# Folding four states at a time, in a selective-scan kernel of 16 layers

## The chip, the cores and the metric

The kernel runs on one core of a Trainium2 chip. The metric is the device time of one execution in microseconds (us); it is 16410.44 us as the median of three runs (16390.57 to 16411.66).

## The reference

Images are embedded as patches (16 x 16 pixels with four shifted copies), joined with text tokens to 16 sequences of 324 tokens with 192 features, and normed. Then come 16 Mamba layers, a shared expert, and a mixture of 16 experts. The change touches only the layers. One layer, cut to what is computed:

```
h = rmsnorm(x) * w;  u, z = split(in_w @ h)               # 384 channels each
u = silu(causal_conv(u) + b)                               # 4 taps, per channel
dt_r, Bm, Cm = split(x_proj @ u)                           # 48, 16, 16
dt = softplus(dt_proj @ dt_r + dt_b);  A = -exp(A_log)     # A: 384 channels x 16 states
for t: h = exp(dt_t * A) * h + dt_t * u_t * B_t            # 16 states per channel
       y_t = sum over n of h[:, n] * C_t[n]  + u_t * D
x = x + out_w @ (y * silu(z))
```

## The kernel before

A **unit** is one sequence in one layer; there are 16 x 16 = 256, and `UNITS` of them run in a loop, two a turn. The recurrence is laid out with 128 partitions = 32 channels x 4 states and 972 elements = 3 x 324 tokens (`IT` x `L`). So a unit is 16 **steps** n = 0 to 15. I call the tile of step s "state s", as the code does; it holds 128 (channel, state) pairs, and four consecutive steps s use the strips r = s mod 4 of the output partitions.

Each step has this chain, one engine after the other:

- ScalarE, **decay** (`se_decay`, line 596): three exponentials from `dt_rep` into a bank pair of PSUM; two such buffers, so decay s waits for scan s - 2.
- GpSimd, **dbu** (`ge_dbu`, 814): `dtu_rep` times `b_rep`; four buffers, so dbu s waits for scan s - 4.
- VectorE, **scan** (`ve_scan`, 764): the recurrence along the tokens into one of eight tiles `h`.
- **product** with C: on VectorE with C from PSUM (`ve_product`, 773) one step later, or for the states in `ON_POOL` on GpSimd with C from SBUF (`ge_product`, 821), issued after dbu s + 4.
- PE, **sum** (`te_sum`, 449): a matmul with the 128 x 32 matrix `fold` adds 128 rows to 32 output partitions of `y_ps`. One call takes two states, so two of the four strips.

Beside it, every engine carries the projections of later units, which a planner of fixed places puts into the steps: for unit u the z projection of u + 1 (`te_z`, 478), the u projection (`te_u`, 513), convolution (`te_conv`, 527), x projection (`te_xp`, 547) and dt projection (`te_dt`, 556) of u + 2, and the squares for the norm of u + 3 (`te_ss`, 539). They share one PSUM bank `pj`, so each waits until ScalarE has evicted the one before: z (line 620), u (632), convolution (639), x (683), dt (691, 692). `te_skip` (465) adds u * D into `y_ps`; `te_bcast` (435) writes the C rows of four states over all partitions for the products. `ve_gate` (781) multiplies `y_ps` with silu(z) when all sums of a unit are in; `te_out` (493, 495) is the output projection, evicted at 626. `ve_log_error` (788) and three GpSimd operations (834 to 842) finish softplus.

Every engine runs its queue in the order in which `tensor_step`, `scalar_step`, `vector_step`, `gpsimd_step` and `sync_step` write it, by step n; waits are semaphores. ScalarE at n = 12 loads an activation table, does the SiLU of u and z, and loads the first table back (647, 653, 655); at n = 1 it loads another for two logarithms and returns (725, 729). In `tensor_step` the eight sums of a unit stand at the places `SUM_AT`: the pairs (0,1), (2,3), ... (12,13) at n = 3, 6, 7, 10, 11, 14, 15, and (14,15) at n = 1 of the next unit. The two halves of the skip stand at n = 7 and 10, the output projection at 3 and 4, the u projection at 5 and 6.

Of the kernel before, what the change touches and what calls it, by code (L numbers as in the profile page):

```python
# [35 lines left out]
DRING = 4  # L36
ON_POOL = (3, 7, 11)
EPS = 1e-5
# [263 lines left out]
LOG_SET = "natural_log"  # L302
FREED = 2 + RING + 1 + 1 + 2 + 1


def run_layers(nc, cst, x_T, params, weights, b_rows, dt_rows, dtu_rows):

    ident, ones96, sel_c, fold = cst["ident"], cst["ones96"], cst["sel_c"], cst["fold"]
    with ExitStack() as ctx:
# [112 lines left out]
        def by_vector(u, s):  # L422

            return (N - len(ON_POOL)) * u + sum(i not in ON_POOL for i in range(s + 1)) + 1

        def by_pool(u, s):

            return len(ON_POOL) * u + sum(i in ON_POOL for i in range(s + 1))

# [6 lines left out]

        def te_sum(pe, u, m):

            if m >= -1:
                reached(pe, s_prod, by_vector(u, 2 * m + 1))  # L440
            if 2 * m + 1 in ON_POOL:
                reached(pe, s_pprod, by_pool(u, 2 * m + 1))
            if m == 0:
                reached(pe, s_gate, u + 1)
            for half in range(2):
                for s in (2 * m, 2 * m + 1):
                    r = s % NR
                    src = h[s % RING][:, :, :].rearrange("p i t -> p (i t)")
                    mm = pe.matmul(y_ps[32 * r:32 * r + 32, half, :], fold[:, :], src[:, half * YW:(half + 1) * YW],  # L449
                                   start=(m in (0, 1)), stop=(m % 8 in (6, 7)))  # L450
            mm.then_inc(s_sum, 1)
# [29 lines left out]

        def te_out(pe, u, half, lone=False):

            if half == 0:
                reached(pe, s_gate, u + 1)
                wait(pe, s_wo, 16 * ((u + B - 1) // B + 1))
                if lone:
                    reached(pe, s_dtev, 2 * u + 4)
                else:
                    reached(pe, s_zev, 2 * u + 4)  # L490
            else:
                reached(pe, s_oev, 2 * u + 1)
# [6 lines left out]
        def te_u(pe, k, par, half, scan, b1):  # L499
            if half == 0:  # L500
                reached(pe, s_xn, k + 1)
                wait(pe, s_wu, 16 * (layer(k) + 1))
                if scan:
                    reached(pe, s_oev, 2 * k - 2)
                elif b1:
                    reached(pe, s_zev, 2 * k)
                else:
                    reached(pe, s_lnss, k + 2)
            else:
                reached(pe, s_ur, 2 * k + 1)  # L510
            for it, lo, hi, t in pieces(half):
                for c in range(2):
                    mm = pe.matmul(pj[:, lo:hi], w_u[:, c, it * 128:it * 128 + 128], x_norm[par][:, c, t:t + hi - lo],  # L513
                                   start=(c == 0), stop=(c == 1))
            mm.then_inc(s_u, 1)

        def te_conv(pe, k, half):

            if half == 0:
                wait(pe, s_wc, 16 * (layer(k) + 1))  # L520
                reached(pe, s_ur, 2 * k + 2)
            else:
                reached(pe, s_cvev, 2 * k + 1)
# [36 lines left out]

        SUM_AT = (3, 6, 7, 10, 11, 14, 15, 1)

        def tensor_step(pe, u, par, scan=True, a1=True, b1=True):

            p, k, j = u + 1, u + 2, u + 3
            for n in range(N):
                if scan and n % 4 == 1:
                    te_bcast(pe, u, par, n // 4)
                if n == 0:
                    te_ss(pe, j, b1)  # L570
                if n in (1, 2) and b1:
                    te_z(pe, p, 1 - par, n - 1)
                if n in (3, 4) and scan:
                    te_out(pe, u, n - 3)
                if n in (5, 6) and a1:
                    te_u(pe, k, par, n - 5, scan, b1)
                if n in (8, 9) and a1:
                    te_conv(pe, k, n - 8)
                if n == 12 and a1:
                    te_xp(pe, k, par)  # L580
                if n in (13, 14) and a1:
                    te_dt(pe, k, n - 13)
                for m in (i for i, at in enumerate(SUM_AT) if scan and at == n):
                    te_sum(pe, u, m if n != 1 else -1)
                if n in (7, 10) and scan:
                    te_skip(pe, u, par, (n - 7) // 3)

# [125 lines left out]
        def scalar_step(act, u, par, scan=True, a1=True, b1=True):  # L713
# [5 lines left out]
            for n in range(N):  # L719
# [15 lines left out]
                if n == 2 and b1:  # L735
                    se_softplus(act, p, 2)
                if n in (4, 5) and scan:
                    se_out(act, u, n - 4)
                if n == 4 and b1:
                    se_c_rows(act, p, other)  # L740
                if n == 5 and a1:
                    se_copy_cb(act, k)
                if n in (6, 7) and a1:
                    se_ur(act, k, n - 6)
                if n == 6:
# [30 lines left out]
        def ve_gate(dve, u, par):  # L776

            reached(dve, s_sum, 8 * u + 2)
            reached(dve, s_za, u)
# [11 lines left out]
        def vector_step(dve, u, par, scan=True, a1=True, b1=True):  # L791
            p = u + 1
            other = 1 - par
            for n in range(N):
                if scan:
                    ve_scan(dve, u, n)
                if n == 2 and scan:
                    ve_gate(dve, u, other)
                if scan:
                    if n - 1 not in ON_POOL:  # L800
                        ve_product(dve, u, n - 1)
                if n == 3 and b1:
                    ve_log_error(dve, p)
# [13 lines left out]
        def ge_product(pool, u, s):  # L817

            wait(pool, s_cr[s // NR], 16 * (u + 1))
            reached(pool, s_scan, 16 * u + s + 1)  # L820
            pool.tensor_tensor(h[s % RING][:, :, :], h[s % RING][:, :, :],  # L821
                               c_rep[:, s // NR, :].unsqueeze(1).broadcast_to([128, IT, L]), ALU.mult).then_inc(s_pprod, 1)

# [36 lines left out]
        def sp_store_b(sp, k, par):  # L860
            reached(sp, s_xpev, k + 1)
            for s in s_bq + s_cr:
                wait(sp, s, 16 * (k - 1))
            sp.dma_start(b_rows[par], xp_rows[96:128, :]).then_inc(s_bst, 16)

# [6 lines left out]

        def sp_load_c(sp, u, par, q):
            reached(sp, s_pprod, len(ON_POOL) * u + q + 1)
            sp.sem_inc(s_go, 1)
            wait(sp, s_bst, 16 * (u + 2))
            sp.dma_start(c_rep[:, q, :], b_rows[1 - par, N + 4 * q:N + 4 * q + 4, :].unsqueeze(0).broadcast_to([32, 4, L])
                         ).then_inc(s_cr[q], 16)

# [87 lines left out]
        with nc.Block() as block:  # L967
            @block.sync
            def _(sp):
# [52 lines left out]
                sp.wait_ge(s_bst, 16 * (UNITS + 2))  # L1022
                for s in s_bq + s_cr + s_dtr + s_dur + s_dst:
                    sp.wait_ge(s, 16 * (UNITS + 1))
                sp.wait_ge(s_wu, 16 * (NL + 1))
                sp.wait_ge(s_wc, 16 * (NL + 1))
# [44 lines left out]
            def _(pool):  # L1071
                raise_counts(pool, s_dbu, s_dt, s_xn, s_pprod)
# [780 lines left out]
```

## Time and profile before

| | |
|---|---|
| median of the runs | 16410.44 us |
| the profiled execution's own time | 16389.14 us |
| its span | 16387.3 us |
| PE matmul busy | 13833.0 us, 84% |
| VectorE (DVE) busy | 13770.8 us, 84% |
| GpSimd (POOL) busy | 13369.5 us, 82% |
| ScalarE (ACT) busy | 11352.2 us, 69% |
| mean granted TensorE clock | 0.889 of full |

Times of rows are microseconds from the start of the span. A row of a timeline is a group of like instructions that follow each other: start, duration, engine, source line, operation, output <- inputs, shapes, count; in brackets stands how long the engine had been idle before it and what released it. A float32 matmul call shows as two matmul instructions. Instructions of one engine overlap by about 0.08 us, so starts are the better measure than durations. Matmul ends are modelled.

### The profile page before, as it was taken

How to read it: one execution, taken by the hardware profiler on the slowest of the kernel's cores; microseconds unless marked ns; L12 is line 12 of the kernel's file. 1: busy time of each engine (PE TensorE's matmuls, PEld its weight loads, DVE VectorE, ACT ScalarE, POOL GpSimd, SP SyncE). 2: the span in 40 equal slices, each digit the busy share in tenths (PEclk: the TensorE clock that was granted, in tenths of full speed). 3: DMA queues.
4: the chain of work that ended last, by engine and by line, in shares of the span. 5: the costliest groups of instructions: out<-in, count | busy, mean ns of one | idle time of the engine just before them, and what ended most of it. 6: DMA issues, size and time to landing. Idle time of an engine off the chain costs nothing. (4 is left out here: it accounts for less than half of the span.)

```text
span 16387.3 us, 204104 instructions
## 1 busy us (share of the span) xinstructions
PE 13833.0 (84%) x52202; PEld 6844.4 (42%) x52202; DVE 13770.8 (84%) x9806; ACT 11352.2 (69%) x21632; POOL 13369.5 (82%) x6093
## 2 busy tenths in 40 slices
PE   6888888888888888888888888888888888887689
PEld 4344444444443444444444444443443444444367
DVE  2899899989998998999899899989998998994643
ACT  3777777777777777777777777777777777774111
POOL 1999999999999999999999999999999999990023
PEclk7888888988999998888888988989998888887799
DMA  2333333333333333333333333333333333331022
GB/s 71 117 110 110 110 118 106 114 114 115 107 114 116 110 109 113 116 106 114 115 113 108 113 116 110 109 113 115 106 114 116 112 108 114 115 110 40 11 51 58
DMA packets 714623, 1703.38 MB, mean 104 GB/s; under 512 B 89050, under 2 KB 369607, under 8 KB 714307
## 3 DMA queue, kind: packets, MB, share of 16 engines
q1 hardware_dynamic: 693810, 1685.70, 30.8%
q0 software_dynamic: 19968, 15.98, 0.6%
q14 instruction: 109, 0.89, 0.0%
q10 hardware_dynamic: 720, 0.55, 0.0%
q8 instruction: 16, 0.26, 0.0%
HBM read 1415.12 MB, written 286.74 MB: 104 GB/s over the span
## 5 line engine op out<-in xcount | busy, mean ns | idle before, releaser
L814 POOL TENSOR_TENSOR dbu<-dtu_rep,b_rep 128x972 f32<-128x972 f32 x4096 | 9140.3, 2250 | 1307.6 <-DVE h L764 1282.5
L764 DVE TENSOR_TENSOR_SCAN h<-ps,dbu 128x972 f32<-128x972 f32 x4096 | 8851.4, 2171 | 1073.8 <-ACT ps L596 1072.5
L596 ACT ACTIVATE ps<-dt_rep,A_cur 128x323 f32<-128x323 f32 x12288 | 5882.9, 521 | 1015.7 <-DVE h L764 752.5
L449 PE MATMUL ps<-h,fold 128*32 128x486 f32 x16400 | 4221.9, 696 | 97.9 <-DVE h L773 53.0
L773 DVE TENSOR_TENSOR h<-h,ps 128x972 f32<-128x972 f32 x3329 | 3797.1, 1141 | 1.2 <-PE ps L435 1.2
L449 PEld LDWEIGHTS ps<-h,fold 128*32 128x32 f32 x16400 | 881.1, 125 | 2694.5 <-issue 2173.1
L821 POOL TENSOR_TENSOR h<-h,c_rep 128x972 f32<-128x972 f32 x768 | 1961.8, 2554 | 0.0
L527 PE MATMUL ps<-u_raw,w_cv 128*128 128x162 f32 (+7 forms) x8256 | 1802.5, 372 | 96.2 <-ACT u_pre L639 94.7
L527 PEld LDWEIGHTS ps<-u_raw,w_cv 128*128 128x128 f32 x8256 | 1348.0, 190 | 525.9 <-ACT u_pre L639 227.1
L556 PE MATMUL ps<-xp_rows,w_dt 49*128 49x162 f32 (+1 forms) x2064 | 808.3, 529 | 660.2 <-ACT dt L692 334.2
L478 PE MATMUL ps<-x_norm,w_z 96*128 96x324 f32 (+1 forms) x4112 | 1320.9, 481 | 1.4 <-ACT rstd L665 0.7
L435 PE MATMUL ps<-c_rows,sel_c 16*128 16x324 f32 x2048 | 835.7, 488 | 524.8 <-DVE h L773 523.7
L1611 POOL DMA_INDIRECT e_rows<-n_rows,e_ix x96 | 96.9, 1010 | 1301.4 <-issue 1205.7
L513 PE MATMUL ps<-x_norm,w_u 96*128 96x324 f32 (+1 forms) x4128 | 989.2, 383 | 193.2 <-ACT u_raw L632 187.4
L478 PEld LDWEIGHTS ps<-x_norm,w_z 96*128 96x128 f32 x4112 | 869.7, 244 | 631.3 <-issue 557.7
L495 PE MATMUL ps<-y_gated,w_o 128*96 128x324 f32 x3084 | 925.8, 436 | 0.0
L513 PEld LDWEIGHTS ps<-x_norm,w_u 96*128 96x128 f32 x4128 | 666.3, 191 | 508.3 <-ACT u_raw L632 251.0
L556 PEld LDWEIGHTS ps<-xp_rows,w_dt 49*128 49x128 f32 x2064 | 425.1, 242 | 941.9 <-ACT xp_rows L683 459.5
L626 ACT COPY x_T<-ps 96x324 f32 (+1 forms) x514 | 218.2, 424 | 835.1 <-PE ps L495 835.1
L547 PE MATMUL ps<-u_act,w_x 128*128 128x324 f32 x1548 | 491.4, 454 | 359.9 <-ACT u_act L647 352.9
L435 PEld LDWEIGHTS ps<-c_rows,sel_c 16*128 16x128 f32 x2048 | 300.3, 183 | 941.7 <-DVE h L773 663.9
L639 ACT COPY u_pre<-ps 128x486 f32<-128x486 f32 x516 | 288.2, 559 | 545.7 <-PE ps L527 545.7
(170 smaller groups left out, 14767.0 us busy)
## 6 DMA issues: line engine op xcount, KB each, us to landing
dtu_rep<-dtu_rows SPq DMA_DIRECT2D x1028, 486.0 KB, 3.9
dt_rep<-dt_rows SPq DMA_DIRECT2D x1028, 486.0 KB, 6.5
b_rep<-b_rows SPq DMA_DIRECT2D x1028, 162.0 KB, 2.6
dt_rows<-dt SPq DMA_DIRECT2D x257, 486.0 KB, 2.7
dtu_rows<-dtu SPq DMA_DIRECT2D x257, 486.0 KB, 2.7
c_rep<-b_rows SPq DMA_DIRECT2D x771, 162.0 KB, 5.6
w_cv<-in_w_cv SPq DMA_DIRECT2D x17, 768.0 KB, 7.6
b_rows<-xp_rows SPq DMA_DIRECT2D x258, 40.5 KB, 6.4
```

Of the source, the lines that this page charges most:

```text
L435: pe.matmul(c_ps, sel_c[64:80, q, :], c_rows[par][64:80, :], start=True, stop=True).then_inc(s_cbc, 1)
L449: mm = pe.matmul(y_ps[32 * r:32 * r + 32, half, :], fold[:, :], src[:, half * YW:(half + 1) * YW], start=(m in (0, 1)), stop=(m % 8 in (6, ...
L478: mm = pe.matmul(pj[:, lo:hi], w_z[:, c, it * 128:it * 128 + 128], x_norm[par][:, c, t:t + hi - lo], start=(c == 0), stop=(c == 1))
L495: mm = pe.matmul(pj[0:HC, 0:L], w_o[:, it, half * HC:(half + 1) * HC], y_gated[:, it, :], start=False, stop=(it == IT - 1))
L513: mm = pe.matmul(pj[:, lo:hi], w_u[:, c, it * 128:it * 128 + 128], x_norm[par][:, c, t:t + hi - lo], start=(c == 0), stop=(c == 1))
L527: mm = pe.matmul(pj[:, lo + skip:hi], w_cv[:, it * KC + KC - 1 - back, :], u_raw[:, it * L + t + skip - back:it * L + t + hi - lo - back], ...
L556: mm = pe.matmul(pj[:, lo:hi], w_dt[:, it * 128:it * 128 + 128], xp_rows[0:RB, t:t + hi - lo], start=True, stop=True)
L596: ins = act.activation(decay[s % 2][:, it * L + 1:(it + 1) * L], dt_rep[:, s % NR, it, 1:L], ACT.Exp, scale=A_cur[:, it * N + s:it * N + s ...
L764: dve.tensor_tensor_scan(h[s % RING][:, :, :].rearrange("p i t -> p (i t)"), decay[s % 2], dbu[s % DRING][:, :, :].rearrange("p i t -> p ( ...
L773: dve.tensor_tensor(h[s % RING][:, :, :], h[s % RING][:, :, :], c_ps.unsqueeze(1).broadcast_to([128, IT, L]), ALU.mult).then_inc(s_prod, 1)
L814: pool.tensor_tensor(dbu[s % DRING][:, :, :], dtu_rep[:, r, :, :], b_rep[:, q, :].unsqueeze(1).broadcast_to([128, IT, L]), ALU.mult).then_ ...
L821: pool.tensor_tensor(h[s % RING][:, :, :], h[s % RING][:, :, :], c_rep[:, s // NR, :].unsqueeze(1).broadcast_to([128, IT, L]), ALU.mult).t ...
```

## The change

One sum now takes four states, all four strips, at n = 6, 10, 13 and at n = 2 of the next unit, so four calls with eight matmuls instead of eight with four. GpSimd makes the products of states 1, 5 and 13 instead of 3, 7 and 11; the last is made in the next unit. The u projection (n = 3, 4) goes ahead of the output projection (n = 5, 6); both halves of the skip run at n = 7. The gate stands after scan 3 instead of scan 2, the log error after product 3. ScalarE's evictions and the loads of C move along.

```diff
-ON_POOL = (3, 7, 11)
+ON_POOL = (1, 5, 13)
...
-        def te_sum(pe, u, m):
-
-            if m >= -1:
-                reached(pe, s_prod, by_vector(u, 2 * m + 1))
-            if 2 * m + 1 in ON_POOL:
-                reached(pe, s_pprod, by_pool(u, 2 * m + 1))
-            if m == 0:
+        def te_sum(pe, u, q):
+
+            reached(pe, s_prod, by_vector(u, 4 * q + 3))
+            if (4 * q + 1) % N in ON_POOL:
+                reached(pe, s_pprod, by_pool(u, 4 * q + 1))
+            if q == 0:
                 reached(pe, s_gate, u + 1)
             for half in range(2):
-                for s in (2 * m, 2 * m + 1):
-                    r = s % NR
-                    src = h[s % RING][:, :, :].rearrange("p i t -> p (i t)")
+                for r in range(NR):
+                    src = h[(4 * q + r) % RING][:, :, :].rearrange("p i t -> p (i t)")
                     mm = pe.matmul(y_ps[32 * r:32 * r + 32, half, :], fold[:, :], src[:, half * YW:(half + 1) * YW],
-                                   start=(m in (0, 1)), stop=(m % 8 in (6, 7)))
+                                   start=(q == 0), stop=(q < 0))
...
-        def te_out(pe, u, half, lone=False):
+        def te_out(pe, u, half, a1=True, b1=True):
...
-                if lone:
+                if a1:
+                    reached(pe, s_ur, 2 * u + 6)
+                elif b1:
+                    reached(pe, s_zev, 2 * u + 4)
+                else:
                     reached(pe, s_dtev, 2 * u + 4)
-                else:
-                    reached(pe, s_zev, 2 * u + 4)
...
-                if scan:
-                    reached(pe, s_oev, 2 * k - 2)
-                elif b1:
+                if b1:
                     reached(pe, s_zev, 2 * k)
...
-        def te_conv(pe, k, half):
+        def te_conv(pe, k, half, scan):
 
             if half == 0:
+                if scan:
+                    reached(pe, s_oev, 2 * k - 2)
...
-        SUM_AT = (3, 6, 7, 10, 11, 14, 15, 1)
-
...
+                if n in (2, 6, 10, 13) and scan:
+                    te_sum(pe, u, (n - 6) // 4 if n < 13 else 2)
                 if n in (1, 2) and b1:
                     te_z(pe, p, 1 - par, n - 1)
-                if n in (3, 4) and scan:
-                    te_out(pe, u, n - 3)
-                if n in (5, 6) and a1:
-                    te_u(pe, k, par, n - 5, scan, b1)
+                if n in (3, 4) and a1:
+                    te_u(pe, k, par, n - 3, b1)
+                if n in (5, 6) and scan:
+                    te_out(pe, u, n - 5, a1, b1)
+                if n == 7 and scan:
+                    te_skip(pe, u, par, 0)
+                    te_skip(pe, u, par, 1)
...
-                for m in (i for i, at in enumerate(SUM_AT) if scan and at == n):
-                    te_sum(pe, u, m if n != 1 else -1)
-                if n in (7, 10) and scan:
-                    te_skip(pe, u, par, (n - 7) // 3)
...
-                if n in (4, 5) and scan:
-                    se_out(act, u, n - 4)
+                if n in (6, 7) and scan:
+                    se_out(act, u, n - 6)
...
-                if n in (6, 7) and a1:
-                    se_ur(act, k, n - 6)
+                if n in (4, 5) and a1:
+                    se_ur(act, k, n - 4)
...
-            if s % 2 == 0:
-                reached(dve, s_sum, 8 * u + s // 2 - 1)
+            if s % 4 == 0:
+                reached(dve, s_sum, 4 * u + s // 4)
...
-                if n == 2 and scan:
+                if n == 3 and scan:
                     ve_gate(dve, u, other)
...
-                if n == 3 and b1:
+                if n == 4 and b1:
                     ve_log_error(dve, p)
...
-                    if n - 4 in ON_POOL:
-                        ge_product(pool, u, n - 4)
+                    if (n - 4) % N in ON_POOL:
+                        ge_product(pool, u if n >= 4 else u - 1, (n - 4) % N)
...
-        def sp_load_c(sp, u, par, q):
-            reached(sp, s_pprod, len(ON_POOL) * u + q + 1)
+        def sp_load_c(sp, u, par, at):
+
+            s = ON_POOL[at]
+            reached(sp, s_pprod, by_pool(u - 1, s))
             sp.sem_inc(s_go, 1)
-            wait(sp, s_bst, 16 * (u + 2))
...
+            wait(sp, s_bst, 16 * (u + 1))
...
             p = u + 1
+            if scan:
+                sp_load_c(sp, u, par, len(ON_POOL) - 1)
             for q in range(NQ):
...
-                for q in range(len(ON_POOL)):
-                    sp_load_c(sp, u, par, q)
+                for at in range(len(ON_POOL) - 1):
+                    sp_load_c(sp, p, 1 - par, at)
...
+                pool.memset(c_rep[:, :, :], 0.0).then_inc(s_free, 1)
                 pool.wait_ge(s_free, FREED)
                 all_units(gpsimd_step, pool)
+                ge_product(pool, UNITS - 1, ON_POOL[-1])
```

## Rows read from the trace of the kernel before

**Rows 1.** The gate's line over the whole span: its instructions and their idle time.

```profile
L781 DVE TENSOR_TENSOR y_gated<-ps,z_act x257: 1169/1171/1172, 377.3 to 14785.9; 128x972 f32<-128x972 f32 x129
...
  PE ps L449: 358.4, 251
```

**Rows 2.** Timeline of VectorE, end of one unit and start of the next.

```profile
8001.78 1.14 DVE L773 TENSOR_TENSOR h<-h,ps 128x972 f32<-128x972 f32 x1
8002.84 2.17 DVE L764 TENSOR_TENSOR_SCAN h<-ps,dbu 128x972 f32<-128x972 f32 x1
8004.93 1.14 DVE L773 TENSOR_TENSOR h<-h,ps 128x972 f32<-128x972 f32 x1
...
8014.93 2.18 DVE L764 TENSOR_TENSOR_SCAN h<-ps,dbu 128x972 f32<-128x972 f32 x1 [3.62 <-ACT ps L596]
...
8035.64 1.17 DVE L781 TENSOR_TENSOR y_gated<-ps,z_act 128x972 f32<-128x972 f32 x1 [2.65 <-PE ps L449]
...
8037.80 2.17 DVE L764 TENSOR_TENSOR_SCAN h<-ps,dbu 128x972 f32<-128x972 f32 x1
...
8040.95 2.39 DVE L788 SCALAR_TENSOR_TENSOR dtu<-u_pre,dtu 128x972 f32<-128x972 f32 x1
```

**Rows 3.** Timeline of ScalarE over the same stretch.

```profile
8005.85 1.44 ACT L596 ACTIVATE ps<-dt_rep,A_cur 128x323 f32<-128x323 f32 x3
8008.47 1.28 ACT L647 ACT_TABLE_LOAD   x1 [1.18 <-PE ps L465]
...
8016.68 0.58 ACT L691 ACTIVATE exp_x<-ps 128x486 f32<-128x486 f32 x1
...
8019.43 0.57 ACT L691 ACTIVATE exp_x<-ps 128x486 f32<-128x486 f32 x1 [0.38 <-PE ps L556]
...
8021.40 1.44 ACT L596 ACTIVATE ps<-dt_rep,A_cur 128x323 f32<-128x323 f32 x3 [0.80 <-DMA dt_rep<-dt_rows]
...
8029.25 1.44 ACT L596 ACTIVATE ps<-dt_rep,A_cur 128x323 f32<-128x323 f32 x3
8032.05 0.56 ACT L620 COPY z_pre<-ps 128x486 f32<-128x486 f32 x1 [1.37 <-PE ps L478]
...
8033.98 1.43 ACT L596 ACTIVATE ps<-dt_rep,A_cur 128x323 f32<-128x323 f32 x3
```

**Rows 4.** Timeline of PE matmuls, the same unit and the next.

```profile
8013.31 0.81 PE L435 MATMUL ps<-c_rows,sel_c 16*128 16x324 f32 x2
8015.40 1.08 PE L556 MATMUL ps<-xp_rows,w_dt 49*128 49x324 f32 x4 [1.28 <-ACT xp_rows L683]
...
8028.41 3.61 PE L478 MATMUL ps<-x_norm,w_z 96*128 96x324 f32 x8
8031.95 3.45 PE L449 MATMUL ps<-h,fold 128*32 128x486 f32 x8
...
8038.03 0.78 PE L493 MATMUL ps<-x_T,ident 96*96 x2 [0.79 <-ACT z_pre L620]
...
8040.38 1.83 PE L449 MATMUL ps<-h,fold 128*32 128x486 f32 x8
...
8072.58 1.79 PE L556 MATMUL ps<-xp_rows,w_dt 49*128 49x324 f32 x4 [1.23 <-ACT xp_rows L683]
...
8077.59 4.42 PE L449 MATMUL ps<-h,fold 128*32 128x486 f32 x16
```

**Rows 5.** Windows: length, busy us of PE, PEld, DVE, ACT, POOL; granted clock; DMA.

```profile
8011.50:8018.10 6.60, 4.03 (x14) 2.32 (x15) 3.17 (x3) 6.56 (x13) 6.60 (x4) 1.00 0.78 245
8018.30:8021.50 3.20, 3.20 (x11) 0.84 (x13) 3.20 (x3) 2.02 (x6) 3.20 (x3) 0.50 0.92 333
...
8025.00:8028.40 3.40, 0.73 (x2) 0.29 (x2) 3.40 (x3) 3.35 (x5) 2.50 (x2) 1.00 0.23 71
8028.50:8035.20 6.70, 6.70 (x16) 2.85 (x16) 4.45 (x3) 5.32 (x11) 6.70 (x4) 0.50 0.00 0
```

**Rows 6.** Timeline of GpSimd, its longest wait of the unit.

```profile
8040.05 2.26 POOL L814 TENSOR_TENSOR dbu<-dtu_rep,b_rep 128x972 f32<-128x972 f32 x1 [4.57 <-DVE h L764]
```

More of the change, by code:

```diff
@@ L302 @@
 LOG_SET = "natural_log"
-FREED = 2 + RING + 1 + 1 + 2 + 1
+FREED = 2 + RING + 1 + 1 + 2 + 1 + 1
 def run_layers(nc, cst, x_T, params, weights, b_rows, dt_rows, dtu_rows):
@@ L422, in by_vector @@
         def by_vector(u, s):
+            if s < 0:
+                return by_vector(u - 1, s + N)
             return (N - len(ON_POOL)) * u + sum(i not in ON_POOL for i in range(s + 1)) + 1
         def by_pool(u, s):
-            return len(ON_POOL) * u + sum(i in ON_POOL for i in range(s + 1))
+            if s < 0:
+                return by_pool(u - 1, s + N)
+            return len(ON_POOL) * u + sum(i in ON_POOL for i in range(s + 1)) + 1
         def te_bcast(pe, u, par, q):
@@ L497, in te_out, with te_u @@
             mm.then_inc(s_out, 1)
-        def te_u(pe, k, par, half, scan, b1):
+        def te_u(pe, k, par, half, b1):
             if half == 0:
@@ L570, in tensor_step @@
                     te_ss(pe, j, b1)
+                if n in (2, 6, 10, 13) and scan:
+                    te_sum(pe, u, (n - 6) // 4 if n < 13 else 2)
                 if n in (1, 2) and b1:
                     te_z(pe, p, 1 - par, n - 1)
-                if n in (3, 4) and scan:
-                    te_out(pe, u, n - 3)
-                if n in (5, 6) and a1:
-                    te_u(pe, k, par, n - 5, scan, b1)
+                if n in (3, 4) and a1:
[5 more added lines that the diff above has]
+                    te_skip(pe, u, par, 1)
                 if n in (8, 9) and a1:
-                    te_conv(pe, k, n - 8)
+                    te_conv(pe, k, n - 8, scan)
                 if n == 12 and a1:
@@ L776, in ve_gate @@
         def ve_gate(dve, u, par):
-            reached(dve, s_sum, 8 * u + 2)
+            reached(dve, s_sum, 4 * u + 1)
             reached(dve, s_za, u)
@@ L817, in ge_product @@
         def ge_product(pool, u, s):
-            wait(pool, s_cr[s // NR], 16 * (u + 1))
+            at = ON_POOL.index(s)
+            reached(pool, s_cr[at], 16 * (u + 1))
             reached(pool, s_scan, 16 * u + s + 1)
             pool.tensor_tensor(h[s % RING][:, :, :], h[s % RING][:, :, :],
-                               c_rep[:, s // NR, :].unsqueeze(1).broadcast_to([128, IT, L]), ALU.mult).then_inc(s_pprod, 1)
+                               c_rep[:, at, :].unsqueeze(1).broadcast_to([128, IT, L]), ALU.mult).then_inc(s_pprod, 1)
         def ge_x_norm(pool, j, par):
@@ L861, in sp_store_b @@
             reached(sp, s_xpev, k + 1)
-            for s in s_bq + s_cr:
+            for s in s_bq:
                 wait(sp, s, 16 * (k - 1))
+            for s in s_cr:
+                sp.sem_inc(s_go, 1)
+                reached(sp, s, 16 * (k - 1))
+                sp.sem_inc(s_go, 1)
             sp.dma_start(b_rows[par], xp_rows[96:128, :]).then_inc(s_bst, 16)
@@ L871, in sp_load_b @@
                          ).then_inc(s_bq[q], 16)
-        def sp_load_c(sp, u, par, q):
-            reached(sp, s_pprod, len(ON_POOL) * u + q + 1)
+        def sp_load_c(sp, u, par, at):
+            s = ON_POOL[at]
+            reached(sp, s_pprod, by_pool(u - 1, s))
             sp.sem_inc(s_go, 1)
-            wait(sp, s_bst, 16 * (u + 2))
-            sp.dma_start(c_rep[:, q, :], b_rows[1 - par, N + 4 * q:N + 4 * q + 4, :].unsqueeze(0).broadcast_to([32, 4, L])
-                         ).then_inc(s_cr[q], 16)
+            wait(sp, s_bst, 16 * (u + 1))
+            n = N + s // NR * 4
+            sp.dma_start(c_rep[:, at, :], b_rows[par, n:n + 4, :].unsqueeze(0).broadcast_to([32, 4, L])
+                         ).then_inc(s_cr[at], 16)
         def sp_store_dt(sp, p, which):
@@ L1022, in _ @@
                 sp.wait_ge(s_bst, 16 * (UNITS + 2))
-                for s in s_bq + s_cr + s_dtr + s_dur + s_dst:
+                for s in s_bq + s_dtr + s_dur + s_dst:
                     sp.wait_ge(s, 16 * (UNITS + 1))
+                for s in s_cr[:-1]:
+                    reached(sp, s, 16 * (UNITS + 1))
+                reached(sp, s_cr[-1], 16 * UNITS)
                 sp.wait_ge(s_wu, 16 * (NL + 1))
@@ L1038, in _ @@
                               start=True, stop=False)
-                te_sum(pe, 0, -2)
                 all_units(tensor_step, pe)
                 te_sum(pe, UNITS, -1)
-                te_out(pe, UNITS, 0, lone=True)
-                te_out(pe, UNITS, 1, lone=True)
+                te_out(pe, UNITS, 0, a1=False, b1=False)
+                te_out(pe, UNITS, 1, a1=False, b1=False)
             @block.scalar
@@ L1071, in _ @@
             def _(pool):
-                raise_counts(pool, s_dbu, s_dt, s_xn, s_pprod)
+                raise_counts(pool, s_dbu, s_dt, s_xn, s_pprod, *s_cr)
                 for i in range(2):
```

## The prediction

> **What bounds the kernel now.** I read the page's engine shares first: PE, DVE and POOL are all busy for most of the span and none of them always, so the question is who waits for whom inside one unit (one sequence in one layer; there are 256). The gate product on line 781 runs once a unit, and its first and last start put the mean unit at (14785.9 - 377.3) / 256 = 56.28 us [rows 1]. All of the change lies in this stretch, 14409 us of the 16387 us span.
>
> Next the timeline of VectorE [rows 2]. A scan follows its predecessor's start by 2.09 us if nothing holds it (8002.84 to 8004.93), a product by 1.06 us (8001.78 to 8002.84), gate and one product take 2.16, the log error 2.32 (its 2.39 less the same overlap). Without a wait a unit is 16 x 2.09 + 13 x 1.06 + 1.08 + 2.32 = 50.6 us. The other 5.7 us are waits in two places: scan 13 waits 3.62 us for ScalarE's decay 13, and the gate waits for the fold sum, 2.65 us in this unit and 358.4 / 257 = 1.4 us on average [rows 1, 2].
>
> Then ScalarE's own queue between them [rows 3]: decay 12, table load, SiLUs, table load, decay 13, decays 14 and 15 with the dt evictions between, decay 0 of the next unit, softplus and logarithm, decay 2, the z eviction, decay 3. So I cut the unit at two marks: **E**, the end of scan 10 (8002.84 + 2.17 = 8005.01), and the start of the next unit's scan 3 (8037.80). From scan 3 to E VectorE has no wait: 8 x 2.09 + 5 x 1.06 + 2.32 = 24.3 us. From E to scan 3, which I call X, it took 32.8 us here, and 56.28 - 24.34 = 31.9 on average. In X ScalarE is the longer queue, so X is what the change must shorten.
>
> **The part from scan 3 to E, after.** The gate now follows scan 3 (+1.08), and of products 2 to 8 VectorE does six instead of five (+1.06), since 3 and 7 come back from GpSimd and 5 goes there: 26.5 us. This is 2.1 us more, and it comes off X, as the number of products a unit is still 13 and 3. The part stays without waits if ScalarE keeps up. The output projection now stands behind broadcast 1, which waits for product 3, and ScalarE holds decay 7 back until its first half is evicted. One output half takes PE 8040.38 - 8038.03 = 2.4 us [rows 4]. From scan 3: product 3 ends at 7.5, broadcast to 8.2, the output half to 10.7, its eviction and the weighted x to 12.2, decay 7 to 13.6. Scan 7 is due at 14.9, so 1.3 us are left. I cost it at nothing; at half clock the output half would take twice as long and cost about 1 us.
>
> **X, after, step by step, from E = 0.**
> 1. Decay 12 started 0.84 us after E, behind the second convolution eviction [rows 3]. Product 7 on VectorE gives the convolution 1.06 us more between scans 8 and 10, so this 0.84 goes.
> 2. The table load at 8008.47 waited 1.18 us for the skip matmuls of line 465 [rows 3]. Both halves of the skip now run at n = 7, directly behind the output projection and ahead of the convolution, and the convolution ends before E. The wait goes; it would be back only if the skip came later than the convolution does.
> 3. Decay 13 ended at 8014.91 (scan 13 starts at 8014.93). New: 14.91 - 5.01 - 0.84 - 1.18 = 7.9. VectorE is due at scan 13 after products 9, 10, 11 and scans 11, 12: 3 x 1.06 + 2 x 2.09 = 7.4. The stall falls from 3.6 to 0.5 us, and it is 11 returning to VectorE that fills a third of it.
> 4. What is late next is the dt projection. It is queued on PE behind broadcast 3 and the sum of states 8 to 11, both of which wait for product 11 on VectorE; before, product 11 was GpSimd's, the broadcast went at 8013.31 and the sum came later [rows 4]. Product 11 ends at 7.4, the broadcast takes it to 8.25 (0.81 less overlap), the sum to 10.0, dt half 0 (1.08) to 11.1. ScalarE is ready for it at 16.68 - 5.01 - 2.02 = 9.65. A new wait of 1.45 us on ScalarE; behind it stand decay 15, decay 0 and all that follows. Decay 15 ends at 13.5, scan 15 was due at 13.2.
> 5. Old waits that this swallows: 0.38 us for dt half 1 and 0.80 us for the dt_rep transfer [rows 3]; the transfer is still issued behind dbu 15, which was not moved, and decay 0 now comes at 14.5 instead of 16.4 less the 2.0 of steps 1 and 2, so it may keep a few tenths of its wait. From decay 0 to the end of decay 2: 29.25 + 1.44 - 21.40 = 9.3, so 23.8.
> 6. The z eviction: old wait 1.37 us, with z at half clock (3.61 us) [rows 3, 4]. Scan 0 starts at 16.65, product 15 ends at 19.9, broadcast to 20.7, z half 0 to 24.3: wait 0.5; with a broadcast at half clock 1.0; at full clock none (half of 3.61). From there to the end of decay 3: 33.98 + 1.43 - 32.05 = 3.4.
> 7. So decay 3 is ready at 27.2 at full clock, at 27.7 to 28.2 with z at half clock. The old gate wait is gone from X: the sum -1 is twice as many states, but has until scan 3 has ended; at half clock it ends near 27.8 against a gate at 30.
>
> X + 26.5 is the unit: **53.7 us** at full clock throughout, **54.5 us** with z at half clock, against 56.28.
>
> **The sum of four strips** has no row of its own. The nearest: a sum of two states, eight instructions, takes 1.83 us at full clock and 3.45 at half [rows 4]. If strips overlap only in pairs, sixteen take twice that; if all four do, once. The row at 8077.59 holds two sums on different pairs of strips, sixteen instructions in 4.42 us at half clock, the second begun about a microsecond late: four strips did run together. I take 1.83 and 3.45, and keep 3.66 and 6.9 for the range. PE so loses 4 x 1.83 = 7.3 us of work a unit, which by itself buys nothing, as PE was not last in X.
>
> **The clock.** Granted clock is 0.50, 1.2 GHz, in 8018.3 to 8021.5 and in 8028.5 to 8035.2. Before the first, PE was busy 4.03 of 6.60 us, before the second 0.73 of 3.40 [rows 5]. After the change PE does nothing from the sum of states 4 to 7 (ends near E + 1) to the x projection (E + 4.5), and only one group before E + 7.4; then it idles again from about 14 to 20, as the sums of states 10 to 13 no longer stand there. So z should be at half clock in nearly each unit, and the dt stretch in some. Now dt half 0 is seen at 1.08 us in one unit and at 1.79 in the next [rows 4]; there it cost nothing. If all of step 4 is at half clock: broadcast 1.2, sum 3.45, dt 1.8, so 13.9 instead of 11.1, product 15 and z go along, X = 31.0 and the unit 57.5. If the clock comes back within the sum, about 56.3. I take 56.8 as the mean of such units, and one unit in three: (2 x 54.5 + 56.8) / 3 = 55.3.
> The Trainium skill (TensorE: Matmul & The Clock Gate, Why this matters for your kernels) says that pauses between bursts of matmuls bring the engine back to half rate, and asks to keep it occupied. It speaks against taking work off PE ahead of the dt projection; the trace agrees as far as rows 5 go. By that rule taken strictly all units would be the 57.5 of the third rival below.
> The same page (Part 3, What overlaps and what doesn't) has matmuls start and end in program order. If PE could pull dt half 0 ahead of the sum instead, step 4 would have no wait and the unit would be nearer 53. In every row here PE keeps its order, so the sum goes by order.
>
> **The rest.** SP's load of C for state 13 now heads its step and waits for GpSimd's product 13 of the unit before; behind it stands the load of B's first rows, which waits for dbu 3, made later on GpSimd anyway: nothing. Three C loads a unit, as before. GpSimd makes 16 + 3 + 3 operations of 2.2 us and one of 1.6 either way, 50 us, and idled 4.57 us before the dbu at 8040.05 [rows 6]: with a unit of 55 us it still has 4 to 5. The log error still starts 1 us behind the dbu that overlaps it, so I leave it at 2.39; without GpSimd beside it it could be 1.2 us shorter, and behind a late dbu 1 us longer. The extra memset and the last product are some 5 us once.
>
> **Sum.** (55.27 - 56.28) x 256 = -259 us, +5: 16389 - 254 = 16135 us against the profiled execution, which lies 21 us under the median of the runs shown. **Predicted 16140 us.**
>
> **Rivals.**
> - **Clock stays up** (or z is never late): 53.7 a unit, -660 us, 15730. For it: the four-strip sum is dense work. Against: the two pauses.
> - **Strips overlap in pairs only**: step 4 becomes 1.8 us longer, the unit 56.3 to 56.6, 16390 to 16480: no change. Against it stands 8077.59.
> - **Slower: dt behind the sum at half clock in most units.** The wait of ScalarE between decays 14 and 15 grows from 1.45 to 4.3 us; it decides once that wait and the z wait together pass about 4.1 us (X = 29.8), which is when more than two units in three have it. 57 to 57.6 a unit: 16570 to 16730.
> - **GpSimd or the output projection becomes last** from scan 3 to E: up to 1.5 us a unit on top, 16140 to 16520.
>
> **Chances.** Forecast (15900 to 16330) 0.43, clock up 0.14, pairs 0.09, slower by dt 0.26, GpSimd or output 0.08. Faster by over 0.2% (33 us, about what a measurement tells from none): 0.39 + 0.14 + 0.02 + 0.05 = 0.60. Slower: 0.02 + 0.04 + 0.25 + 0.02 = 0.33. Within: 0.07. Range for 8 in 10: from just inside the full-clock case, 15790, to half-way into the slow rival, 16640; the forecast's own range is 15900 to 16330.
>
> **What would show it.** Idle before scan 13 about 0.5 us; no wait of the table load of line 647 on line 465; a new wait of ScalarE's line 691 on line 556, 1.4 us or up to 4; no wait before the gate; scans 2 and 3 waiting for line 596 instead; sixteen instructions of line 449 in about 1.9 us; mean granted clock of the layers below 0.89. The prediction is wrong if line 691's wait is near 4 us throughout, or if the gate or scan 4 still waits for PE, or if products 1, 5 and 13 hold a sum up.

## The result, and the profile after

The change made the kernel slower: 16629.99 us as the median of four runs (16615.15 to 16633.19), against 16407.94 us before (four runs, 16390.57 to 16411.66). The ratio is 1.0136, with a 95% interval of 1.0118 to 1.0153. The prediction was 16140 us with a range to 16640; it had faster at 0.60 and slower at 0.33. The time lies inside the range, 10 us from its upper end, and on the wrong side.

The gate's line, as in [rows 1], gives the mean unit: (15010.2 - 383.1) / 256 = 57.14 us against 56.28. That is +0.86 x 256 = 220 us, nearly all of 16631.4 - 16387.3 = 244.

```profile
L784 DVE TENSOR_TENSOR y_gated<-ps,z_act x257: 1142/1144/1170, 383.1 to 15010.2; 128x972 f32<-128x972 f32 x129
...
  PE ps L451: 3.6, 1
```

The gate wait is gone (358.4 us before, 3.6 now). The page's group of the scans (busy, mean ns, idle before them and its releaser) shows what came instead: before, they idled 1073.8 us, of which 1072.5 for decay.

```profile
L767 DVE TENSOR_TENSOR_SCAN h<-ps,dbu 128x972 f32<-128x972 f32 x4096 | 8909.7, 2175 | 1597.6 <-ACT ps L599 1585.5
```

The units now repeat in fours: 57.66, 57.79, 57.88 and 55.36 us between gates. I call the units of 55.36 us fast and the others slow. VectorE's timeline of one fast unit (first five rows) and one slow one, to set beside [rows 2]: in the fast unit scan 10, whose end is the mark E, and scans 13, 15, 2 and 3; in the slow unit scans 13, 15, 2 and 3; last, scan 7 of the unit behind it:

```profile
8010.31 2.17 DVE L767 TENSOR_TENSOR_SCAN h<-ps,dbu 128x972 f32<-128x972 f32 x1
...
8020.43 2.18 DVE L767 TENSOR_TENSOR_SCAN h<-ps,dbu 128x972 f32<-128x972 f32 x1 [0.60 <-ACT ps L599]
...
8026.09 2.18 DVE L767 TENSOR_TENSOR_SCAN h<-ps,dbu 128x972 f32<-128x972 f32 x1 [0.32 <-ACT ps L599]
...
8036.95 2.18 DVE L767 TENSOR_TENSOR_SCAN h<-ps,dbu 128x972 f32<-128x972 f32 x1 [1.32 <-ACT ps L599]
8040.93 2.18 DVE L767 TENSOR_TENSOR_SCAN h<-ps,dbu 128x972 f32<-128x972 f32 x1 [1.80 <-ACT ps L599]
...
8075.85 2.18 DVE L767 TENSOR_TENSOR_SCAN h<-ps,dbu 128x972 f32<-128x972 f32 x1 [0.59 <-ACT ps L599]
...
8083.74 2.18 DVE L767 TENSOR_TENSOR_SCAN h<-ps,dbu 128x972 f32<-128x972 f32 x1 [2.57 <-ACT ps L599]
...
8094.22 2.18 DVE L767 TENSOR_TENSOR_SCAN h<-ps,dbu 128x972 f32<-128x972 f32 x1 [0.94 <-ACT ps L599]
8098.59 2.18 DVE L767 TENSOR_TENSOR_SCAN h<-ps,dbu 128x972 f32<-128x972 f32 x1 [2.19 <-ACT ps L599]
...
8113.91 2.18 DVE L767 TENSOR_TENSOR_SCAN h<-ps,dbu 128x972 f32<-128x972 f32 x1 [0.33 <-ACT ps L599]
```

Scan 13's stall fell from 3.62 to 0.6 us, and other scans took it up. ScalarE's timeline, beside [rows 3]: decay 13, dt half 0 and z of the fast unit, output half 0, then dt half 0 and z of the slow one.

```profile
8018.96 1.44 ACT L599 ACTIVATE ps<-dt_rep,A_cur 128x323 f32<-128x323 f32 x3
...
8023.69 0.58 ACT L694 ACTIVATE exp_x<-ps 128x486 f32<-128x486 f32 x1 [1.50 <-PE ps L560]
...
8037.55 0.56 ACT L623 COPY z_pre<-ps 128x486 f32<-128x486 f32 x1 [0.63 <-PE ps L480]
...
8053.55 0.42 ACT L629 COPY x_T<-ps 96x324 f32 x1 [4.54 <-PE ps L499]
...
8081.35 0.58 ACT L694 ACTIVATE exp_x<-ps 128x486 f32<-128x486 f32 x1 [3.75 <-PE ps L560]
...
8095.21 0.56 ACT L623 COPY z_pre<-ps 128x486 f32<-128x486 f32 x1 [1.02 <-PE ps L480]
```

PE's timeline, beside [rows 4], shows why 1.50 became 3.75: x projection, broadcast 3, the four-strip sum and dt half 0 of the fast unit, then of the slow one, each followed by broadcast 0 and z half 0. Between the two stand the matmuls of output half 0 (8050.34) and output half 1 (8055.62).

```profile
8016.99 1.90 PE L551 MATMUL ps<-u_act,w_x 128*128 128x324 f32 x6 [3.47 <-ACT u_act L650]
8019.89 0.81 PE L439 MATMUL ps<-c_rows,sel_c 16*128 16x324 f32 x2 [1.01 <-DVE h L776]
8020.63 1.84 PE L451 MATMUL ps<-h,fold 128*32 128x486 f32 x16
8022.40 1.08 PE L560 MATMUL ps<-xp_rows,w_dt 49*128 49x324 f32 x4
...
8032.53 1.44 PE L439 MATMUL ps<-c_rows,sel_c 16*128 16x324 f32 x2 [2.69 <-DVE h L776]
8033.90 3.61 PE L480 MATMUL ps<-x_norm,w_z 96*128 96x324 f32 x8
...
8050.34 2.96 PE L499 MATMUL ps<-y_gated,w_o 128*96 128x324 f32 x6
...
8055.62 1.80 PE L499 MATMUL ps<-y_gated,w_o 128*96 128x324 f32 x6
...
8072.40 2.90 PE L551 MATMUL ps<-u_act,w_x 128*128 128x324 f32 x6 [3.47 <-ACT u_act L650]
8075.31 1.44 PE L439 MATMUL ps<-c_rows,sel_c 16*128 16x324 f32 x2
8076.68 3.45 PE L451 MATMUL ps<-h,fold 128*32 128x486 f32 x16
8080.06 1.08 PE L560 MATMUL ps<-xp_rows,w_dt 49*128 49x324 f32 x4
...
8090.19 1.44 PE L439 MATMUL ps<-c_rows,sel_c 16*128 16x324 f32 x2 [2.99 <-DVE h L776]
8091.56 3.61 PE L480 MATMUL ps<-x_norm,w_z 96*128 96x324 f32 x8
```

The same stretches by granted clock, as in [rows 5]; the mean over the span fell from 0.889 to 0.809:

```profile
8000.00:8025.00 25.00, 18.73 (x95) 10.86 (x94) 24.21 (x16) 19.24 (x37) 23.65 (x12) 1.00 0.42 141
8025.50:8039.00 13.50, 9.68 (x24) 4.24 (x26) 11.85 (x8) 12.40 (x23) 13.50 (x7) 0.50 0.41 133
...
8053.00:8073.00 20.00, 16.04 (x86) 9.41 (x85) 19.68 (x13) 15.42 (x30) 19.92 (x11) 1.00 0.29 106
8073.50:8080.00 6.50, 6.49 (x22) 1.74 (x20) 5.91 (x5) 4.08 (x8) 5.11 (x3) 0.50 0.84 253
8080.00:8083.30 3.30, 2.00 (x12) 1.24 (x8) 1.18 (x1) 1.95 (x5) 3.30 (x3) 1.00 0.81 319
8083.50:8097.00 13.50, 9.32 (x27) 4.45 (x30) 11.72 (x7) 12.31 (x22) 11.32 (x6) 0.50 0.28 86
```

In the slow unit PE had idled 3.47 us for the SiLU; the clock fell to half 0.8 us into the x projection, and broadcast and sum ran at half. The pause alone doesn't decide it: the fast unit has the same 3.47 us ahead of the same projection, and there the clock stayed up. Between 8000 and 12000 us it fell in 52 of 69 units, three in four. No run shows what spares the fourth.

### The profile page after: what moved, and what is told of

Its sections match the earlier page's. It is cut to its first block and busy times, and to the rows that moved or that the text cites. A ratio compares the mean times of both kernels' runs of the same rounds, so it can differ in the third digit from the quotient of the medians.

```text
span 16631.4 us, 203353 instructions
## 1 busy us (share of the span) xinstructions
PE 13009.7 (78%) x52202; PEld 6846.6 (41%) x52202; DVE 13828.1 (83%) x9806; ACT 11310.3 (68%) x21632; POOL 13141.1 (79%) x6095
## 5 line engine op out<-in xcount | busy, mean ns | idle before, releaser
L451 PE MATMUL ps<-h,fold 128*32 128x486 f32 x16400 | 2461.6, 729 | 4.6 <-DVE h L776 4.6
L439 PE MATMUL ps<-c_rows,sel_c 16*128 16x324 f32 x2048 | 1111.4, 631 | 1275.3 <-DVE h L776 1274.4
L825 POOL TENSOR_TENSOR h<-h,c_rep 128x972 f32<-128x972 f32 x769 | 1730.4, 2250 | 3.7 <-DVE h L767 3.7
L480 PE MATMUL ps<-x_norm,w_z 96*128 96x324 f32 (+1 forms) x4112 | 1419.3, 507 | 1.4 <-ACT rstd L668 0.7
L551 PE MATMUL ps<-u_act,w_x 128*128 128x324 f32 x1548 | 618.6, 547 | 896.0 <-ACT u_act L650 889.0
L499 PE MATMUL ps<-y_gated,w_o 128*96 128x324 f32 x3084 | 1293.3, 572 | 0.0
L451 PEld LDWEIGHTS ps<-h,fold 128*32 128x32 f32 x16400 | 507.8, 132 | 1482.4 <-issue 1477.3
L694 ACT ACTIVATE exp_x<-ps 128x486 f32<-128x486 f32 x516 | 295.9, 573 | 865.0 <-PE ps L560 865.0
L543 PE MATMUL ps<-sq,ones 96*96 96x324 f32 x1036 | 640.4, 773 | 307.6 <-ACT dt L695 303.3
L560 PE MATMUL ps<-xp_rows,w_dt 49*128 49x162 f32 (+1 forms) x2064 | 610.6, 417 | 335.5 <-ACT dt L695 334.2
```

Source lines behind the costliest of these rows:

```text
L439: pe.matmul(c_ps, sel_c[64:80, q, :], c_rows[par][64:80, :], start=True, stop=True).then_inc(s_cbc, 1)
L480: mm = pe.matmul(pj[:, lo:hi], w_z[:, c, it * 128:it * 128 + 128], x_norm[par][:, c, t:t + hi - lo], start=(c == 0), stop=(c == 1))
L543: mm = pe.matmul(pj[0:HC, 0:L], ones96[:, :], sq[:, c, :], start=(c == 0), stop=(c == 1))
```

## The experiments

Each was timed in three rounds against the kernel before, whose median was 16388 to 16399 us in them; a ratio is to that median, that of the change to 16407.94. The mean unit is from the first and last gate, as in [rows 1]; "dt wait" is ScalarE's wait for line 556's matmuls per unit, summed over both halves, in 8000 to 12000 us of the span.

| kernel | time us | ratio, 95% interval | unit us | dt wait us | clock |
|---|---|---|---|---|---|
| before | 16407.94 | 1 | 56.28 | 0.8 | 0.889 |
| the change | 16629.99 | 1.0136 [1.0118, 1.0153] | 57.14 | 3.3 | 0.809 |
| a_dt | 16828.86 | 1.0263 [1.0246, 1.0280] | 57.98 | 4.4 | 0.800 |
| a_busy2 | 15982.77 | 0.9750 [0.9734, 0.9766] | 54.61 | 1.7 | 0.915 |
| a_busy1 | 16400.33 | 1.0002 [0.9993, 1.0012] | 56.27 | 1.7 | 0.836 |
| a_dt_busy2 | 16842.26 | 1.0270 [1.0253, 1.0287] | 57.98 | 4.2 | 0.851 |
| a_dt2 | 16202.35 | 0.9882 [0.9866, 0.9899] | 55.46 | 1.8 | 0.820 |
| a_dt2_busy2 | 15974.78 | 0.9743 [0.9727, 0.9759] | 54.64 | 1.1 | 0.880 |
| a_out | 16806.42 | 1.0248 [1.0231, 1.0266] | 57.93 | 3.0 | 0.809 |
| a_dt2_out | 16269.08 | 0.9924 [0.9907, 0.9940] | 55.75 | 1.1 | 0.828 |
| a_dt2_out_busy2 | 16091.98 | 0.9814 [0.9798, 0.9831] | 54.95 | 0.8 | 0.889 |
| a_dt2_out_busy3 | 16821.73 | 1.0266 [1.0249, 1.0283] | 57.90 | 0.7 | 0.828 |
| b_skip | 16085.98 | 0.9812 [0.9795, 0.9828] | 55.03 | 1.1 | 0.881 |
| b_skip_busy | 16031.68 | 0.9774 [0.9757, 0.9790] | 54.89 | 0.9 | 0.913 |

VectorE's wait before a scan, us a unit, as the mean over the whole units between 8000 and 12000 us, tells where each edit worked. In the kernel before the gate waits 1.44 us beside them.

| kernel | scan 13 | 15 | 0 | 2 | 3 | 7 and 8 |
|---|---|---|---|---|---|---|
| before | 3.62 | 0 | 0 | 0.41 | 0 | 0 |
| the change | 0.59 | 2.12 | 0 | 1.06 | 2.07 | 0.22 |
| a_busy1 | 0.60 | 0.32 | 0.09 | 1.12 | 2.01 | 1.07 |
| a_busy2 | 0.60 | 0.32 | 0.08 | 1.01 | 1.10 | 0.31 |
| a_dt2 | 0.65 | 0.15 | 0.65 | 0.92 | 1.29 | 0.68 |
| a_dt2_busy2 | 0.59 | 0 | 0 | 1.13 | 1.10 | 0.81 |

### The clock: zero matmuls in PE's pauses

```diff
+        def te_busy(pe, count):
+
+            for i in range(count):
+                pe.matmul(y_ps[:, i % 2, :], zero[:, :], A_all[:, 0:YW], start=False, stop=False)
...
                 if n == 0:
                     te_ss(pe, j, b1)
+                    if scan:
+                        te_busy(pe, 4)
...
+                if n == 11 and scan:
+                    te_busy(pe, 3)
```

a_busy2 has both places:

> The changed kernel with order untouched, but PE given matmuls with zero weights that add nothing to y_ps: three between the sum of states 4 to 7 and the x projection, four behind the squares. This is extra work on PE, 5.7 us a unit at full clock. Theory: the pauses lower the clock and the clock makes three of four units slow, so granted clock goes from 0.81 to over 0.95, all units have the 1.5 us wait for dt and none for z, and the unit is 53.9 to 54.3 us, the time about 15850. Rival, order alone: 16600 or more, since PE only has more to do. Rival, the added work delays the x projection: dt wait 2 to 4 us, over 16630.

PE got seven more matmul calls a unit, and the kernel became 647 us faster. The wait for dt half 0 is 1.50 us in each unit, z is waited for no more, as this row of ScalarE in a_busy2 and the absence of line 480's counterpart among its waits say:

```profile
8015.50 0.58 ACT L704 ACTIVATE exp_x<-ps 128x486 f32<-128x486 f32 x1 [1.50 <-PE ps L566]
...
8044.37 0.43 ACT L639 COPY x_T<-ps 96x324 f32 x1 [4.74 <-PE ps L505]
```

It was 130 us slower than expected. The clock still fell (0.915, not over 0.95): at the output projection in every unit, where scan 7's 0.31 us a unit are some 80 us, and behind the dt projection, which nothing here prices. With the first place alone:

> The changed kernel, order untouched, with only the three zero matmuls ahead of the x projection. Theory: it is the half clock at the dt projection that makes three units of four slow; with it up there, every unit is like the fast one, 55.4 us, z still at half clock: time about 16180. Rival: the later pause, ahead of z, matters as much: 16400 or more.

16400 us, as its rival had it. The dt wait is the same 1.7 us, so the three matmuls there take away what the half clock added to it; of the 1.7 us, 1.5 are left in each unit. Scan 15's wait fell by 1.80 us a unit, from 2.12 to 0.32, the size that was expected. Only 0.87 us of it reached the unit, as scans 7 and 8 now wait 1.07 instead of 0.22 us for the output projection. The four matmuls ahead of z give the other 1.66 us (54.61 against 56.27), 0.91 of them at scan 3 and 0.76 at scans 7 and 8: the pause ahead of z matters as much, and part of it by where the clock then falls.

### The place in the queue

a_dt puts dt half 0 ahead of broadcast 3 and the sum; `te_dt(pe, k, 0)` is called first at n = 13.

> The changed kernel with dt half 0 issued at n = 13 ahead of broadcast 3 and of the four-strip sum of states 8 to 11. Theory: the loss sits in ScalarE's wait for that projection (1.5 us where PE is at full clock, 3.75 at half), so order decides: the wait of line 694 falls to under 0.5 us in every unit, scan 15 no longer waits, the z projection at half clock becomes last, and the unit goes from 57.1 to about 55.2 us, the time to about 16130. Rival, clock alone (PE would be as late in any order): about 16600. Rival, output projection alone (ScalarE waits 4.5 us for it at n = 6): no change, 16630.

16829 us: all three were wrong. ScalarE's timeline in a_dt shows where the wait went, to half 1, because broadcast and sum now stand between the halves, and VectorE waits for the late broadcast:

```profile
8015.25 0.58 ACT L696 ACTIVATE exp_x<-ps 128x486 f32<-128x486 f32 x1 [0.91 <-PE ps L560]
...
8021.15 0.57 ACT L696 ACTIVATE exp_x<-ps 128x486 f32<-128x486 f32 x1 [3.52 <-PE ps L560]
```
```profile
8016.46 1.17 DVE L778 TENSOR_TENSOR h<-h,ps 128x972 f32<-128x972 f32 x1 [1.69 <-PE ps L439]
```

The same order with the zero matmuls:

> Both edits together: dt half 0 ahead of the sum, and the zero matmuls in both pauses. Theory: neither dt nor z is waited for, ScalarE's own queue is what is left of X, the unit about 52.7 us, the time about 15500. If order alone mattered, the same as with the dt edit alone (16130); if the clock alone mattered, the same as with the matmuls alone (15850).

16842 us, no gain either, and none of the three; the wait for half 1 stays (4.2 us a unit in both halves), and the clock falls in that stretch still. So a_dt2 moved the sum, not the projection:

```diff
-                if n in (2, 6, 10, 13) and scan:
-                    te_sum(pe, u, (n - 6) // 4 if n < 13 else 2)
+                if n in (2, 6, 10) and scan:
+                    te_sum(pe, u, (n - 6) // 4)
...
                 if n in (13, 14) and a1:
                     te_dt(pe, k, n - 13)
+                if n == 14 and scan:
+                    te_sum(pe, u, 2)
```

> The changed kernel with the four-strip sum of states 8 to 11 moved behind both dt halves (n = 14), broadcast 3 left where it is. With the sum merely behind half 0 the wait moved to half 1 (3.5 us), since the sum then stood between the halves. Theory, place in the queue: both waits of line 694 fall under 1 us, the wait for z grows to 1 to 2 us as ScalarE is early, unit 55 to 56 us, time about 16180. Rival, the clock alone: PE at half clock keeps it at 16600. Rival, scan 0 of the next unit now waits for the late sum by over 1 us: 16450 or more.

16202 us: the time that the theory had, with the clock no higher than 0.820. The move of one sum behind two calls is 428 us, and it turns the change from 1.4% slower into 1.2% faster. Scan 15's wait fell from 2.12 to 0.15 us a unit, though the clock still fell behind the x projection in 58 of 71 units. The details were not all as foretold: ScalarE still waits for dt half 0 by over 1 us in 57 of 72 units (1.8 us a unit in both halves, against 3.3), the wait for z fell, from 2.1 to 0.9 us a unit, and scan 0 waits 0.65 us for the late sum, part of what the last rival had. ScalarE in a_dt2, in a unit without a wait for dt half 0; the rows are dt half 1 and z half 0:

```profile
8022.26 0.58 ACT L696 ACTIVATE exp_x<-ps 128x486 f32<-128x486 f32 x1 [0.75 <-PE ps L560]
8033.81 0.56 ACT L625 COPY z_pre<-ps 128x486 f32<-128x486 f32 x1 [0.90 <-PE ps L480]
```

Do the two cures add?

> The same with the zero matmuls in both pauses (three ahead of the x projection, four behind the squares). Theory: queue place and clock add up; the matmuls alone gave 54.6 us a unit, of which the 1.5 us dt wait is then gone: 53.3 us, time about 15650. If only the clock mattered, 15980 as with the matmuls alone.

They do not: 15975 beside 15983 with the matmuls alone. The wait for dt fell from 1.7 to 1.1 us a unit and scan 15's 0.32 us went, but scan 7 waits 0.81 instead of 0.31 us, with the output projection at half clock in every unit. Scans 2 and 3 wait 1.0 to 1.1 us each with either, for decays 2 and 3. It is the fastest kernel of the study, level with a_busy2.

### The output projection

a_out calls output half 0 ahead of broadcast 1, as ScalarE's longest wait of all, 4.54 us above, is for it.

> The changed kernel with output half 0 issued ahead of broadcast 1 instead of behind it, all else as changed. In the changed kernel ScalarE waits up to 4.5 us for this half at n = 6, and scan 7 then waits 0.3 us for decay 7 in three units of four. Theory (dt place and clock): only those 0.3 us go, about 16570. Rival, the output projection is what made the change slow: 16400 or less.

16806 us, slower, and neither had it. The wait is shorter, the first convolution half is done earlier, and PE then idles for broadcast 2; the second half comes at half clock. PE in a_out:

```profile
8044.78 3.42 PE L531 MATMUL ps<-u_raw,w_cv 128*128 128x324 f32 x16
8050.23 0.81 PE L439 MATMUL ps<-c_rows,sel_c 16*128 16x324 f32 x2 [2.03 <-DVE h L778]
8051.14 5.22 PE L531 MATMUL ps<-u_raw,w_cv 128*128 128x162 f32 x16
```

Its eviction is late, and scan 13 waits 2.0 instead of 0.6 us in every unit. On top of a_dt2, without and with the zero matmuls, and with two more of them in this new pause:

> The sum of states 8 to 11 behind both dt halves, and output half 0 ahead of broadcast 1. Theory: 16202 less the 0.2 to 0.3 us that scan 7 waits, about 16140; if PE's pause moves and the clock falls elsewhere, within 100 us of 16202 on either side.

> The two moves and the zero matmuls in both pauses. With the matmuls and the dt move alone (15975) the clock fell at the output projection instead, and scan 7 waited 0.3 to 1.25 us for decay 7. Theory: that wait goes, 0.8 us a unit, about 15780, the fastest of all. Rival: the clock falls once more in another place and takes it back, 15950 or more.

> The two moves and the zero matmuls, with two more of these behind the first convolution half. Without them PE idles 1.6 to 2 us there for broadcast 2, the clock is at half in the second convolution half (5.2 us instead of 3.5), its eviction is 1.7 us late and scan 13 waits 2.0 us instead of 0.6. Theory: the clock stays up there, scan 13 is back at 0.6, unit 53.2 to 53.7 us, time about 15720, the fastest. Rival: the two matmuls delay broadcast 2 or the clock falls elsewhere: 15980 or more.

The first came to 16269, within the 100 us that it was given, the second to 16092, as its rival had it. Against the same kernels without the move of output half 0 (a_dt2, a_dt2_busy2) they lost 67 and 117 us, and scan 13 waits 2.3 and 2.1 us a unit instead of 0.6. The third fell through: with the last pause filled, the half clock came to lie on the second half of the u projection, output half 0, broadcast 1 and the sum behind it, 13.4 us in each unit, and once more on dt half 1 and the sum behind it. The units repeat at 58.03, 58.03, 58.02 us; scans 8, 13 and 3 wait 1.4, 1.2 and 1.6 us, and two products 2.3 in sum. Windows of a_dt2_out_busy3:

```profile
8006.50:8019.70 13.20, 11.93 (x53) 6.15 (x51) 10.98 (x8) 12.24 (x22) 13.20 (x7) 1.00 0.06 15
8020.10:8033.50 13.40, 12.61 (x35) 5.11 (x34) 11.44 (x8) 5.82 (x14) 10.83 (x6) 0.50 0.23 87
```

### One part alone, on the kernel before

b_skip calls both skip halves at n = 7 and changes nothing else.

```diff
-                if n in (7, 10) and scan:
-                    te_skip(pe, u, par, (n - 7) // 3)
+                if n == 7 and scan:
+                    te_skip(pe, u, par, 0)
+                    te_skip(pe, u, par, 1)
```

> The kernel before with one part of the change alone: both halves of the skip at n = 7. Theory: the 1.18 us wait of the table load goes, the stall before scan 13 falls from 3.62 to about 2.4, and the rest of the unit keeps its waits: unit 55.1 us, time about 16105. Rival: the gate, which waits for PE's sum at half clock, or a changed pattern of the clock takes it back: 16300 to 16400.

16086 us, 1.9% faster: on the kernel before this part of the change is worth 322 us (312 against the median of its own rounds). The table load follows decay 12 without a wait, and scan 13 waits 2.29 us instead of 3.62:

```profile
8006.24 1.45 ACT L597 ACTIVATE ps<-dt_rep,A_cur 128x323 f32<-128x323 f32 x3
8007.70 1.28 ACT L648 ACT_TABLE_LOAD   x1
```

The other waits did not stay as they were, though they cancel: the gate's fell from 1.44 to 0.25 us a unit, scan 2's rose from 0.41 to 1.19, and products wait 0.44. That the time came out near 16105 is in part luck.

This one call, moved on the kernel before, gives a faster kernel than the whole change with its sum in the best place found (16086 against 16202). With zero matmuls in both, the changed kernels are 50 to 60 us ahead of b_skip_busy below (15975 and 15983 against 16032), with three more matmul calls. So no run shows what the four-strip sum buys by itself; it was not tried alone, nor the other products on GpSimd, nor the u projection ahead of the output projection.

> The kernel before with both skip halves at n = 7 and four zero matmuls (on two strips) behind the squares. Theory: z and the sum at half clock cost about 1 us a unit at scan 2 and the gate; the unit goes from 54.8 to about 54.0 us, time 15880. Rival: PE has no room there, the added work delays z and broadcast 0: 16100 or more.

Only 54 us more, 150 short of what was expected: what was left of the gate's wait went (0.25 to 0.05 us a unit), but scan 2 still waits 0.8 us a unit for decay 2.

## Why the prediction was wrong

**The removed waits were right.** Decay 13 ended 7.9 us after E, as worked out (8018.96 + 1.44 = 8020.40, less 8010.31 + 2.17 = 8012.48), the table load waits for nothing, scan 13 stalls 0.6 us (0.5 foretold). b_skip shows the skip's share by itself, on the kernel before: 322 us against 305 expected, the 1.3 us of scan 13 as worked out and the rest by cancelling.

**The new wait was right.** The dt wait is 1.50 us at full clock (1.45), 3.75 at half (4.3 for the whole of step 4 at half; dt half 0 itself was back at full, 1.08 us). The z wait is 0.63 us in the fast unit and 1.02 in the slow one. Both have a broadcast at half clock, for which 1.0 was foretold; in the fast unit ScalarE itself came 0.6 us late. a_dt2 shows that the place of the sum causes the wait of VectorE behind it: with the sum last, scan 15's 2.12 us became 0.15 at about the same clock.

**The sum of four strips was right.** Sixteen instructions take 1.84 us at full and 3.45 at half clock; the rival of pairs is out.

**The step that failed** is "one unit in three" for a dt stretch at half clock. It was three in four. I took it from the kernel before, where the dt projection was at half in every other unit, and lowered it, though the same paragraph works out a pause of 3.5 us ahead of the x projection (E + 1 to E + 4.5; 3.47 measured) where the kernel before had 1.4. What one such unit costs was right: 2.4 us, against 56.8 - 54.5 = 2.3. Between 55.4 and 57.8 us a unit, 3/4 - 1/3 is 1.0 us or 256 us. a_busy1 shows the size at scan 15, 1.80 us a unit = 3/4 x 2.4; as half of it came back at scans 7 and 8, the kernel only got back to the time of before. The whole is the third rival, with its mechanism and its place; it had 57 to 57.6 a unit and 0.26. Its turning point, two units in three, fits its own units of 54.5 and 56.8 to 57.5; with the measured ones it lies at (56.3 - 55.4) / 2.4, two in five. Why the clock falls in three units of four, and not in all or in one of two, stays open.

**Two terms were small.** The fast unit is 55.4 us, not 54.5: decay 0 comes 0.6 us later than worked out, behind dt half 1 (a wait of 0.21), the copy of A and a gap of 0.19; so X was 28.45 instead of 28.0. The output projection, priced at nothing, is at half clock in every unit (2.96 us for what takes 1.80 at full) and makes scan 7 wait 0.2 to 0.3 us in three of four; the prediction had named that case and put about 1 us to it. The two are 0.8 of the 0.9 us. 0.9 x 256 = 230 us, and with the 256 this is the difference from 16140 to within 5 us.

**The Trainium skill's rule** on pauses (TensorE: Matmul & The Clock Gate, Why this matters for your kernels) was the better guide, and the trace agrees with it in part. The x projection went to half clock in three units of four and z in all, after pauses of 3.47 and 2.7 to 3.0 us; but one unit in four had the same 3.47 us and stayed at full, and the clock also fell behind shorter pauses: 2.03 us in a_out, and 1.23 us ahead of the dt half 0 that took 1.79 us in the kernel before [rows 4]. I had weighed the rule as a rival and not in the forecast.

## What to carry to other kernels

When an engine with a clock gate is given less work, list its new pauses and price what follows each of them at half rate before crediting anything. A merged operation has one release, that of its last input: look at what is queued behind it, here a projection which needs none of its inputs, and try the merged operation behind it. Then test the parts one at a time: here the move of the skip alone did better than the whole. An edit that takes a wait away moves the pause, so one that is right by itself (output half 0 earlier) can cost 1%.

## What was not expected

Extra matmuls that compute nothing made the kernel 3.9% faster than the change and 2.5% faster than before. And three kernels with different edits and waits (a_dt, a_dt_busy2, a_dt2_out_busy3) settled at 58.0 us a unit (means of two units of 58.03, 58.03 and 58.02), each with the half clock at the same places in every unit, three in a_dt and two in the others. It looks as if unit and clock lock to each other, so that a small edit can jump between patterns: two more matmul calls a unit took a_dt2_out_busy2 from 16092 to 16822 us. That was not tested by itself and stays open, as does whether a_busy2 and a_dt2_busy2 would keep their patterns under another small edit.
